# Strassen's seven block products in the second layer of a two-layer adapter and feed-forward kernel on one Trainium2 core

## The reference

```python
w = weight[adapter_ids]                       # one 512 x 512 matrix per batch
x = einsum('bsi,boi->bso', x, w)              # "z" below
nx = x * rsqrt(mean(x*x) + 1e-5) * ln_w
g = nx @ gate_w.T ; u = nx @ up_w.T           # both 1792 x 512
out = (silu(g) * u) @ down_w.T                # down_w is 512 x 1792
```

## Time and profile before

| | |
|---|---|
| runs | 495.27, 496.51, 498.93 us, median 496.51 |
| profiled execution | 499.74 us, of it span 497.9 us from first to last instruction |
| TensorE busy | 97% of the span, 2115 matmuls |
| VectorE, ScalarE, GpSimd busy | 49%, 30%, 18% |
| mean granted clock | 0.986 |

### The profile page before, as it was taken

One profiled execution on the slowest core, in us unless ns is written; L12 is line 12 of the kernel. 1 busy time (PEld: TensorE's weight loads), 2 busy tenths in 40 slices (PEclk: granted clock), 3 DMA queues, 4 the chain that ended last, 5 costly groups with the idle time before them and its releaser, 6 DMA issues.

```text
span 497.9 us, 5802 instructions
## 1 busy us (share of the span) xinstructions
PE 483.5 (97%) x2115; PEld 393.5 (79%) x2115; DVE 244.2 (49%) x320; ACT 149.4 (30%) x172; POOL 92.0 (18%) x88
## 2 busy tenths in 40 slices
...
GB/s 244 114 28 84 91 102 100 112 112 83 121 74 201 72 268 32 28 84 251 171 0 44 84 42 42 42 59 67 42 42 42 37 37 53 60 37 44 115 44 42
DMA packets 13011, 41.69 MB, mean 84 GB/s; under 512 B 2465, under 2 KB 3889, under 8 KB 11841
## 3 DMA queue, kind: packets, MB, share of 16 engines
...
...
## 4 chain that ended last, share of the span: by engine, by line
PE 89%; issue 3%; DVE 2%; DMA 2%; POOL 1%; ACT 1%; SPq 0%; DVEq 0%; ACTq 0%; POOLq 0%
PE ps L838 29%; PE ps L839 29%; PE ps L842 29%; DMA res<-in_xT 2%; POOL h_lo L362 1%; DVE act_lo L541 1%; ACT h_hi L373 1%; PE ps L978 1%; PE ps L969 1%; PE ps L971 1%; PE ps L970 1%; PE ps L862 0%; PE ps L863 0%; ACT sil L484 0%; DVE sil L770 0%
## 5 line engine op out<-in xcount | busy, mean ns | idle before, releaser
L838 PE MATMUL ps<-h_hi,ring_hi 128*128 128x512 f32 x376 | 146.3, 389 | 0.0
L839 PE MATMUL ps<-h_lo,ring_hi 128*128 128x512 f32 x376 | 146.3, 389 | 0.0
L842 PE MATMUL ps<-h_hi,ring_lo 128*128 128x512 f32 x376 | 119.8, 389 | 0.0
L373 ACT ACTIVATE ring_hi<-raw 128x1024 fp32r<-128x1024 f32 (+3 forms) x41 | 40.5, 988 | 215.5 <-PE ps L842 147.9
L838 PE MATMUL ps<-act_hi,ring_hi 128*128 128x512 f32 x224 | 87.3, 390 | 0.0
L839 PE MATMUL ps<-act_lo,ring_hi 128*128 128x512 f32 x224 | 87.1, 389 | 0.0
L838 PEld LDWEIGHTS ps<-h_hi,ring_hi 128*128 128x128 f32 x376 | 70.6, 188 | 14.7
L839 PEld LDWEIGHTS ps<-h_lo,ring_hi 128*128 128x128 f32 x376 | 70.6, 188 | 14.7
L842 PEld LDWEIGHTS ps<-h_hi,ring_lo 128*128 128x128 f32 x376 | 70.6, 188 | 14.6
L686 DVE TENSOR_TENSOR sil<-sil,ps 128x1024 f32<-128x1024 f32 x25 | 30.5, 1218 | 104.3 <-PE ps L842 104.3
L541 DVE TENSOR_TENSOR ring_lo<-raw,ring_hi 128x1024 fp32r<-128x1024 f32 (+3 forms) x41 | 46.5, 1135 | 64.3 <-ACT ring_hi L373 64.3
...
## 6 DMA issues: line engine op xcount, KB each, us to landing
adapters<-in_w1T SPq DMA_DIRECT2D x7, 1024.0 KB, 6.5
raw<-in_gu SPq DMA_DIRECT2D x14, 512.0 KB, 3.6
...
res<-in_xT SPq DMA_DIRECT2D x3, 512.0 KB, 8.8
...
out_T<-res SPq DMA_DIRECT2D x3, 512.0 KB, 3.8
...
```

Source lines behind the costliest of these rows:

```text
L373: act.activation(dst, src, ACT.Copy).then_inc(done, 1)
L838: pe.matmul(ps[:, bank + hf, :], w_hi, v_hi[:, t], start=first, stop=False)
L839: pe.matmul(ps[:, bank + hf, :], w_hi, v_lo[:, t], start=False, stop=False)
L842: ins = pe.matmul(ps[:, bank + hf, :], w_lo, v_hi[:, t], start=False, stop=last)
```

## The change

The gate/up product is a 2 x 2 block product: gate and up rows by the two halves of the 512 features, and feature halves by token halves. Before, its eight block products are made; after, seven, by Strassen's algorithm in Winograd's form, with 7 x 2 x 3 = 42 matmuls a group. The blocks are combined first: four sums of weight blocks (`sums`, on POOL, 128x256 each, per group), four sums of activation blocks per batch pair (`z_sums`, of batch b with batch b-4, on POOL for b = 4, 5, 6 and on DVE for b = 7). Seven weight blocks and seven activation blocks are split, in place of four and four. Products that share a partial sum are accumulated in one PSUM bank, and ACT copies the bank to SBUF in between (`snap_1`, `snap_2`, `snap_5`), so that a later matmul waits for that copy. DVE then adds (`c_11`, `c_12`, `c_22`) and multiplies (`mul_0`, `mul_1`). The result h1 is stored in fp32 and not split.

The down product is also a 2 x 2 block product (output row halves, odd and even h tiles, token halves), made in seven rounds r of two weight tiles p, 21 matmuls each: 7 x 2 x 21 = 294 in place of 336. Each round splits 2 x 896 columns of weights (`d1_w_hi`, `d1_w_lo`) and 7 tiles of 512 (`d1_b_hi`, `d1_b_lo`, parts of 4 and 3 tiles). POOL makes the sums of weights (128x896) and of h1 (parts of 128x2048 and 128x1536) between rounds; DVE makes one of them. Each round ends with two adds to the residual (`d1_add`).

Memory is laid out anew by hand. The adapter of batch b+2, not b+3, is split in the step of batch b, and the loads of adapters wait for other semaphores. Seven product waits are added on TensorE (for `s_s1`, `s_s2`, `s_s5`, `s_c22` among them), and each operand of a round waits for `s_bhi`, `s_blo`.

The core of the diff (the memory layout, index helpers and most removed lines are left out):

```diff
-CH1 = (7, 7)
+PAIRS = FT1 // 2
+WC = PAIRS * P
 EPS = 1e-5
+B_A11, B_A12, B_A22, B_S1, B_S2, B_S3, B_S4 = range(7)
+W_OF = {1: B_A11, 2: B_A12, 3: B_S4, 4: B_A22, 5: B_S1, 6: B_S2, 7: B_S3}
+Z_T1, Z_T2, Z_T3, Z_T4, Z_B22 = range(5)
+Z_OF = {3: Z_B22, 4: Z_T4, 5: Z_T1, 6: Z_T2, 7: Z_T3}
+BLK = 2 * P
...
+        def z_sums(eng, b):
+            s, n = b % 2, b - 4
+            eng.wait_ge(s_nx, b + 1)
+            if b >= 6:
+                eng.wait_ge(s_nlo, split_count(b - 2))
+            b11, b21 = zf[:, n, 0:BLK], zf[:, n, BLK:2 * BLK]
+            b12, b22 = st_b[:, s, 0:BLK], st_b[:, s, BLK:2 * BLK]
+            t1, t2, t3, t4 = (st_t[:, s, i, :] for i in (Z_T1, Z_T2, Z_T3, Z_T4))
+            eng.tensor_tensor(t1, b12, b11, ALU.subtract).then_inc(s_tz[1], 1)
+            eng.tensor_tensor(t3, b22, b12, ALU.subtract).then_inc(s_tz[3], 1)
+            eng.wait_ge(s_tz[1], n + 1)
+            eng.tensor_tensor(t2, b22, t1, ALU.subtract).then_inc(s_tz[2], 1)
+            eng.wait_ge(s_tz[2], n + 1)
+            eng.tensor_tensor(t4, b21, t2, ALU.subtract).then_inc(s_tz[4], 1)
...
+            for b in range(2, 6):
+                sp.wait_ge(s_htwo, 2 if b % 2 == 0 else 4)
+                load_adapter(b)
             sp.wait_ge(s_z, 1)
+            load_gu1(1, 1)
+            for b in range(6, NBATCH):
+                sp.wait_ge(s_z, b - 3)
+                load_adapter(b)
...
+            raw_free(sp, Q["d1"])
+            for name in ("A11_0", "A11_1", "A21_0"):
+                load_d1(name)
+            raw_free(sp, Q["d1"] + 1)
+            for name in ("A22_0", "A21_1"):
+                load_d1(name)
+            sp.wait_ge(s_hm0, FT1 - 1)
+            sp.wait_ge(s_hm1, FT1 - 1)
+            for name in ("A22_1", "A12_0"):
+                load_d1(name)
+            sp.wait_ge(s_hm0, FT1)
+            sp.wait_ge(s_hm1, FT1)
+            load_d1("A12_1")
...
+                need(pool, s_raw["gu1"][s], (g - s) * 8 + 16)
+                w = raw1[s]
+                a21, a11, a12, a22, s1, s2, s3, s4 = (w[:, i, :] for i in (0, 1, 2, 3, 4, 5, 6, 7))
+                pool.tensor_tensor(s1, a21, a22, ALU.add).then_inc(s_sum[1], 1)
+                pool.tensor_tensor(s3, a11, a21, ALU.subtract).then_inc(s_sum[3], 1)
+                need(pool, s_sum[1], g + 1)
+                pool.tensor_tensor(s2, s1, a11, ALU.subtract).then_inc(s_sum[2], 1)
+                need(pool, s_sum[2], g + 1)
+                pool.tensor_tensor(s4, a12, s2, ALU.subtract).then_inc(s_sum[4], 1)
+            def t_sums(b):
+                z_sums(pool, b)
+            for b in range(4):
                 adapter_lo(b)
+            sums(0, 0)
+            for b in (4, 5):
                 adapter_lo(b)
+            sums(1, 1)
+            adapter_lo(6)
+            t_sums(4)
+            adapter_lo(7)
+            t_sums(5)
+            t_sums(6)
+            with loop(pool, 1, FT1 // 2) as j:
+                for s in range(2):
+                    sums(2 * j + s, s)
+            for p in range(2):
+                a21, a22 = d1_raw[f"A21_{p}"], d1_raw[f"A22_{p}"]
+                pool.wait_ge(s_dw[f"A21_{p}"], 16)
+                pool.wait_ge(s_dw[f"A22_{p}"], 16)
+                pool.tensor_tensor(a21, a21, a22, ALU.add).then_inc(s_ds[1], 1)
+            pool.wait_ge(s_bhi, 2)
+            pool.wait_ge(s_blo, 2)
+            pool.wait_ge(s_hm1, FT1 - 1)
+            b11, b12 = d1_block(0, 0, 1), d1_block(0, 1, 1)
+            pool.tensor_tensor(b11, b12, b11, ALU.subtract).then_inc(s_dt[1], 1)
+            for p in range(2):
+                pool.wait_ge(s_ds[1], p + 1)
+                pool.wait_ge(s_wlo, Q["d1"] + p + 1)
+                s1, a11 = d1_raw[f"A21_{p}"], d1_raw[f"A11_{p}"]
+                pool.tensor_tensor(a11, s1, a11, ALU.subtract).then_inc(s_ds[2], 1)
+            for part in range(2):
+                pool.wait_ge(s_hm1, FT1)
+                pool.wait_ge(s_blo, 3 + part)
+                t1, b22 = d1_block(0, 0, part), d1_block(1, 1, part)
+                pool.tensor_tensor(t1, b22, t1, ALU.subtract).then_inc(s_dt[2], 1)
+            for p in range(2):
+                pool.wait_ge(s_ds[2], p + 1)
+                pool.wait_ge(s_wlo, Q["d1"] + 4 + p + 1)
+                s2, a12 = d1_raw[f"A11_{p}"], d1_raw[f"A12_{p}"]
+                pool.tensor_tensor(a12, a12, s2, ALU.subtract).then_inc(s_ds[4], 1)
+            for part in range(2):
+                pool.wait_ge(s_dt1a, 1)
+                b12, b22 = d1_block(0, 1, part), d1_block(1, 1, part)
+                pool.tensor_tensor(b12, b22, b12, ALU.subtract).then_inc(s_dt[3], 1)
+            for p in range(2):
+                pool.wait_ge(s_ds[4], p + 1)
+                pool.wait_ge(s_wlo, Q["d1"] + 6 + p + 1)
+                s2, a22 = d1_raw[f"A11_{p}"], d1_raw[f"A22_{p}"]
+                pool.tensor_tensor(s2, a22, s2, ALU.subtract).then_inc(s_ds[3], 1)
+            for part in range(2):
+                pool.wait_ge(s_dt[2], part + 1)
+                pool.wait_ge(s_blo, 5 + part)
+                t2, b21 = d1_block(0, 0, part), d1_block(1, 0, part)
+                pool.tensor_tensor(b21, b21, t2, ALU.subtract).then_inc(s_dt[4], 1)
...
+            batch_z(0, 0)
+            adapter_hi(2, 0)
+            batch_r(0, 0)
+            adapter_hi(2, 1)
+            for b in range(1, NBATCH):
+                s = b % 2
                 batch_z(b, s)
+                if b + 2 < NBATCH:
+                    adapter_hi(b + 2, 0)
                 batch_r(b, s)
                 batch_n(b - 1, 1 - s)
+                if b + 2 < NBATCH:
+                    adapter_hi(b + 2, 1)
+                if b == 3:
+                    w1_hi(0, 0, s_z, 4)
+                if b == 5:
+                    w1_hi(1, 1, s_z, 2)
+            act.wait_ge(s_nlo, split_count(6))
+            snap_1(0, 0)
+            batch_n(NBATCH - 1, 1)
+            silu_0(0, 0)
+            snap_1(1, 1)
+            snap_5(0, 0)
+            silu_0(1, 1)
+            snap_2(0, 0)
+            silu_1(0, 0)
+            snap_5(1, 1)
+            w1_hi(2, 0, s_p[4], 1)
+            snap_2(1, 1)
+            silu_1(1, 1)
+            def frame(g, s, weights):
+                snap_1(g, s)
+                weights()
+                snap_5(g, s)
+                silu_0(g, s)
+                snap_2(g, s)
+                silu_1(g, s)
...
+            frame(FT1 - 2, 0, lambda: w1_hi(FT1 - 1, 1, s_p[4], FT1 - 2))
+            snap_1(FT1 - 1, 1)
+            for p in range(2):
+                d1_w_hi(0, p)
+            snap_5(FT1 - 1, 1)
+            silu_0(FT1 - 1, 1)
+            d1_b_hi(0, 0)
+            snap_2(FT1 - 1, 1)
+            silu_1(FT1 - 1, 1)
+            d1_b_hi(0, 1)
+            for r in range(1, 7):
+                for p in range(2):
+                    d1_w_hi(r, p)
+                for part in range(2):
+                    d1_b_hi(r, part)
...
+            def w1_lo(g, s):
+                need(dve, s_whi, g + Q["gu1"] + 1)
+                lo(ring1_lo[s], raw1[s][:, 1:8, :].rearrange("p b n -> p (b n)"), ring1_hi[s], s_wlo)
+            def c_11(g, s):
+                need(dve, s_p[2], g + 1)
+                need(dve, s_s1, g + 1)
+                dve.tensor_tensor(snap[s][:, 0, :], ps[:, 3 * s + 1, :], snap[s][:, 0, :], ALU.add).then_inc(s_c11, 1)
...
+            def mul_1(g, s):
+                need(dve, s_silu1, g + 1)
+                need(dve, s_c22, g + 1)
+                dve.tensor_tensor(h_half(g, 1), snap[s][:, 1, :], snap[s][:, 2, :], ALU.mult).then_inc(s_hm1, 1)
+            def d1_w_lo(r, p):
+                dve.wait_ge(s_whi, Q["d1"] + 2 * r + p + 1)
+                hi_, lo_ = d1_ring(r, p)
+                lo(lo_, d1_raw[f"{d1_source[r]}_{p}"], hi_, s_wlo)
+            def d1_b_lo(r, part):
+                dve.wait_ge(s_bhi, 2 * r + part + 1)
+                u = d1_units(r, part)
+                o, hf = d1_place[r]
+                lo(u[:, :, HALF:2 * HALF], d1_block(o, hf, part), u[:, :, 0:HALF], s_blo)
...
+            var(0, 0)
+            norm(0, 0)
+            adapter_lo(2)
+            for b in range(1, NBATCH):
+                s = b % 2
                 var(b, s)
                 weigh(b - 1, 1 - s)
                 norm(b, s)
+                if b + 2 < NBATCH:
+                    adapter_lo(b + 2)
                 n_lo(b - 1, 1 - s)
+                if b == 3:
+                    w1_lo(0, 0)
+                if b == 5:
+                    w1_lo(1, 1)
+            weigh(NBATCH - 1, 1)
+            z_sums(dve, NBATCH - 1)
+            n_lo(NBATCH - 1, 1)
+            c_11(0, 0)
+            c_11(1, 1)
+            c_12(0, 0)
+            c_22(0, 0)
+            mul_1(0, 0)
+            mul_0(0, 0)
+            w1_lo(2, 0)
+            c_12(1, 1)
+            c_22(1, 1)
+            mul_1(1, 1)
+            def frame(g, s, weights, extra=lambda: None):
+                mul_0(g - 1, 1 - s)
+                weights()
+                c_11(g, s)
```

(106 more changed lines are left out.)

471 lines of the change are left out of this document (259 added, 212 removed).

## The result

The changed kernel takes 534.91 us (median of 4 runs, 534.17 to 536.91) where the kernel before takes 496.84 (4 runs beside it): ratio 1.077, 95% interval 1.072 to 1.082. It is 7.7% slower, with 126 matmuls fewer. The profiled execution has a span of 532.6 us and a time of 534.4.

A forecast was written before the change was run, and what follows sets the result against it. TensorE, busy 97%, bounded the kernel before; the POOL/DVE lock would set down. Span 497.9 - 28.6 + 21 (z) + 6.6 + 1.6 + 3 + 31 (down) = 532.5; plus 1.84, times 0.9935: 530.7, said 530, range 500 to 546.

The forecast's parts named there:

- (d): Whole kernel: the main forecast, 530 us, bounds 510 to 543, with the lock setting down; chance 0.80.
- Matmuls removed, 28.6 us: Gate/up and down: 126 matmuls fewer at 0.227 us each save 28.6 us.
- Rival (b): All feeds keep up and the removed matmuls are the result: span 469 to 472, time 469; chance 0.04.
- The lock: DVE work with two SBUF inputs and POOL sums exclude each other, whole instructions at a time; down loses 31 us.
- Rival (a): The lock does not decide, as sums are cheaper or run in gaps: span 493, time 491; chance 0.10.
- Prices of POOL: POOL sums scaled at 2.35 ns a column: 4.8 us for 2048 columns, 41.6 us in down from 433.5 on.
- Turns: Down: DVE gets one instruction between two of POOL's, 22 us; POOL done at 497.1, round 4's splits at 500.5.
- z: Stage 1: first product needing all batches, `p_5(0,0)`, starts at 292; the stage costs 21 us, bounds 13 and 25.
- the walk: Stage 1, walking the engines' lists: product 4 at 251.2, 5 at 257.1, 6 at 265.9, 7 at 274.9, `p_5(0,0)` at 293.6.
- Groups: Gate/up: the wait loop through `snap_2` to `p_7` idles TensorE 0.6 us a group, 6.6 us in all; clock stays.
- Rival (c): Gate/up: the 0.6 us gaps lower the clock, +1.6 us a group, +19 us in all, time 549; chance 0.06.
- From span to median: Whole kernel: 534.2 us times 0.9935, the earlier kernel's median 496.51 against its profiled 499.74, gives 530.7.

The follow-up runs named there:

- run 42: Not a label of a run: in "The groups now run 42 matmuls", run is a verb and 42 the matmuls of a gate/up group.
- experiment 4: Changed kernel with ACT's `snap_2` ahead of `silu_0` in each gate/up group: 530.25 us, ratio 1.063 to the kernel before.
- experiments 1 and 3: Changed kernel, down's POOL sums: in 1 cut to one column each, 505.11 us; in 3 moved to DVE except `ds1` and those ahead of round 1, 516.49 us.
- experiment 5: Kernel before with z's adapters split two batches ahead, not three, and no sums added: 504.9 us, ratio 1.011.
- experiment 7: Changed kernel with the activation sums of batches 4, 5 and 6 in z moved from POOL to DVE: 529.11 us, ratio 1.060.
- experiment 6: Changed kernel with `adapter_lo(7)` ahead of `t_sums(4)` on POOL and ACT's second adapter half ahead of `batch_n`: 537.43 us, ratio 1.077.
- experiment 9: Kernel before with POOL's adapter subtraction cut into two pieces, 496.16 us, ratio 0.9947, or into four, 497.32 us, ratio 0.9967.

## Why the prediction was right

The forecast was (d), span 532.4 and 530 us; the span is 532.6 and the median 534.91. By its steps:

- **Matmuls removed, 28.6 us.** The groups now run 42 matmuls in 9.52 us where nothing waits (experiment 4). Right. Rival (b) needed all feeds to keep up; they don't in z or down.
- **The lock.** Right, and the largest term: down was to lose 31 us with 3 more at the change of stage; without the sums' columns 28.2 come back from `p_5(0,0)` on. Rival (a), that the lock doesn't decide, is refuted by experiments 1 and 3 and by the 4.17 and 2.28 us of one and the same split.
- **Prices of POOL.** I scaled wide sums at 2.35 ns a column: 4.8, 3.6 and 2.1 us for 2048, 1536 and 896. They take 4.46, 3.36 and 1.95, some 2.18 ns a column. That is 38.5 us for the stage (6 x 1.95, 4 x 3.36, 3 x 4.46), not 41.6. The Trainium skill's "GPSIMD Engine Reference", section "3.1 Elementwise — side-by-side cycle accounting", gives 4497 ns for 2048 fp32 columns: closer to the trace than my scaling. A sum of 256 takes 0.73 with the port free, between my bounds of 0.6 and 1.0.
- **Turns.** Right in this kernel: `POOL is done at` 497.1 was the step, measured 495.8; round 4's last split was due at 500.5 and ends at 500.64. Within that, two errors cancel, and that the step came out within 0.2 us is luck. The stage starts later (`d1_b_lo(0,1)` ends at 437.1, not 433.5, of which 2.7 come from z), and POOL needs 58.7 us from there, not 63.6. Of the 4.9, 3.1 are its prices. The rest is in DVE's turns: behind a wait a DVE split takes some 0.13 us less than alone, as the rows of before had it already (0.56 for 0.69, 1.08 for 1.23), and the sum of turns took the full 22 us.
- **z.** 292 was taken for `p_5(0,0)`, and the walk itself said 293.6; it starts at 294.70, 2.7 late, although z's first product started 1.1 us earlier than in the run of before (230.25 against 231.33). The walk was late by no more than 1.7 for any product (`251.2`, `257.1`, `265.9`, `274.9` against 250.11, 256.26, 264.54, 273.20). z loses 23.8 us (294.7 - 5.4 - 265.5), 24.9 counted from its first product. The lookahead is some 5 of them (experiment 5), the late sums on POOL another 5 (experiment 7). The remaining 14 or so (the other sums, the lock in z, the clock) were not taken apart. That `t_sums(4)` ahead of `adapter_lo(7)` causes the last delay was right as a row and wrong as a lever (experiment 6).
- **Groups.** Forecast 0.6 us of idle before `p_7` and a kept clock: a group takes 10.06 us, 0.54 over its matmuls, at a clock of 1.00. The cause, `snap_2` behind `silu_0`, is shown by experiment 4. Rival (c), that these gaps lower the clock, is out.
- **From span to median.** The one step that failed. I multiplied by 0.9935, since the profiled run of before was 0.65% above its median. That is scatter of one execution, not a property of the program: that run's clock was 0.986, and the runs of before at this clock are the slow ones (experiment 9), while the changed kernel's profiled run (534.4) lies 0.5 us from its median. Without the factor the forecast is 534.2, 0.7 us from the result.
